# Attention and expert kernel: queries computed transposed for two tiles at a time, rope rows placed by DMA, slots in group order

## The reference

```python
q_c = layernorm(x) @ W_dq                       # 96 values a row
kv_c = ctx @ W_kvc                              # 64 values a key
scores = (q_nope . k_nope + rope(q_rope) . rope(k_rope)) / sqrt(128 + 64)
good = (k <= seg_id) & (k >= seg_id - 8)        # a band of 9 keys
out = softmax(where(good, scores, -1e30)) @ v @ W_o
x = x + out
gate = layernorm(x) @ gate_w + gate_b           # top 2 of 8
x = x + mean of the two relu(layernorm(x) @ expert_w[e] + expert_b[e])
```

## Time and profile before

| | |
|---|---|
| three runs, us | 395.62, 395.87, 397.86; median 395.87 |
| span of the profiled execution, us | 391.2 |
| around it, by the median | 4.7 |
| busy us: PE, PEld, DVE, ACT, POOL | 354.0, 289.2, 288.3, 264.0, 234.1 |
| share of the span | 90%, 74%, 74%, 67%, 60% |

### The profile page before, as it was taken

The page is one execution under the profiler, slowest core; times in us unless marked ns, Lnnn a source line. Parts: engine busy times, 40 slices in busy tenths (PEclk is TensorE's granted clock), DMA queues, the critical chain, the costliest instruction groups (busy, mean ns, idle before and its releaser), DMA issues.

```text
span 391.2 us, 10358 instructions
## 1 busy us (share of the span) xinstructions
PE 354.0 (90%) x2507; PEld 289.2 (74%) x2507; DVE 288.3 (74%) x1395; ACT 264.0 (67%) x907; POOL 234.1 (60%) x326
## 2 busy tenths in 40 slices
PE   1989999998999999999999999999998788999940
PEld 0856877786688878888878888788886577888730
DVE  2367887788888889888788888888889566444455
ACT  1347777788878878778888788788787544445430
POOL 4616555468976777677677676776764355455500
PEclk9999999999999999999999999999999999999985
DMA  8964040000000000000000000000000354543178
GB/s 277 349 215 188 7 105 3 1 3 29 0 30 1 30 20 7 27 0 27 14 14 27 0 27 0 27 27 0 30 2 28 95 161 131 148 132 121 34 239 316
DMA packets 15093, 28.27 MB, mean 72 GB/s; under 512 B 2892, under 2 KB 10719, under 8 KB 14416
## 3 DMA queue, kind: packets, MB, share of 16 engines
q1 hardware_dynamic: 11408, 20.25, 16.1%
q0 software_dynamic: 2960, 6.94, 5.0%
q10 hardware_dynamic: 688, 0.64, 0.6%
HBM read 17.81 MB, written 10.91 MB: 73 GB/s over the span
## 4 chain that ended last, share of the span: by engine, by line
PE 65%; DVE 12%; issue 10%; POOL 7%; DMA 2%; ACT 2%; DVEq 0%; SPq 0%; POOLq 0%; ACTq 0%
PE psum L1133 11%; PE psum L672 8%; PE psum L673 8%; PE psum L674 8%; PE psum L1090 7%; PE psum L1203 6%; PE psum L1117 5%; POOL prob L1361 2%; DVE x_all L1554 2%; POOL q_sb L1347 2%; PE psum L1180 2%; DVE nsc L1622 2%; DMA wcat<-in_w_kvc 2%; PE psum L369 2%; PE psum L1012 1%
## 5 line engine op out<-in xcount | busy, mean ns | idle before, releaser
L1228 ACT ACTIVATE prob<-nsc,nmax 128x128 f32<-128x128 f32 x256 | 100.8, 396 | 36.3 <-DVE nmax L1622 35.5
L1347 POOL TENSOR_TENSOR q_sb<-rope_a,rope_b 128x256 f32<-128x256 f32 x64 | 47.5, 742 | 59.2 <-DVE rope_b L1585 55.1
L1361 POOL TENSOR_TENSOR prob<-prob,prec 128x512 f32<-128x512 f32 x64 | 67.2, 1050 | 7.4 <-DVE prec L1593 7.4
L1133 PE MATMUL psum<-kT_all,qT 128*128 (+1 forms) x512 | 68.6, 277 | 1.1 <-ACT qT L1271 1.1
L1622 DVE CUSTOM_DVE_ANT_0 nsc<-psum,mask 128x128 f32<-128x128 f32 x256 | 58.6, 284 | 13.0 <-PE psum L1133 13.0
L1133 PEld LDWEIGHTS psum<-kT_all,qT 128*128 128x128 f32 x512 | 62.1, 192 | 2.7 <-ACT qT L1271 2.4
L1415 POOL DMA_INDIRECT halves<-jout,jidx x33 | 32.2, 976 | 30.3 <-DVE jidx L1526 13.7
L1228 ACT ACTIVATION_READ_ACCUMULATOR prob<-nsc,nmax 128x1 f32 x256 | 48.4, 189 | 0.0
L1090 PE MATMUL psum<-ident,q_sb 128*128 128x128 f32 x256 | 41.9, 286 | 2.2 <-POOL q_sb L1347 1.8
L1090 PEld LDWEIGHTS psum<-ident,q_sb 128*128 128x128 f32 x256 | 26.8, 140 | 21.7 <-POOL q_sb L1347 13.6
L1203 PE MATMUL psum<-pT,v_cur 128*64 128x256 f32 x256 | 41.8, 405 | 0.0
(11 more groups left out here) (204 smaller groups left out, 878.1 us busy)
## 6 DMA issues: line engine op xcount, KB each, us to landing
wanted<-slots SPq DMA_DIRECT2D x33, 129.0 KB, 2.4
wo_raw<-in_w_o SPq DMA_DIRECT2D x2, 1024.0 KB, 14.9
we_raw<-in_expert_w SPq DMA_DIRECT2D x1, 2048.0 KB, 7.8
half<-halves SPq DMA_DIRECT2D x4, 512.0 KB, 7.1
x_all<-in_x SPq DMA_DIRECT2D x2, 640.0 KB, 17.4
slots<-pad_row SPq DMA_DIRECT2D x8, 129.0 KB, 3.4
we_raw<-in_ctx_near SPq DMA_DIRECT2D x1, 1024.0 KB, 11.2
out<-x_all SPq DMA_DIRECT2D x2, 512.0 KB, 4.6
```

The source lines that it names most:

```text
L1133: mm = pe.matmul(B_S[r][:, h, :], qT[r][:, h, :], batch_keys, start=True, stop=True)
L1228: e = act.activation(prob[r][:, h, :], nsc[r][:, h, :], ACT.Exp, bias=nmax[r][:, h:h + 1], scale=-1.0, accum_out=psum_h[r][:, h:h + 1])
L1347: pool.tensor_tensor(q_sb[1 - r][:, :, KVC:P], rope_a[1 - r][:], rope_b[1 - r][:], ALU.add).then_inc(m["rope_joined"], 1)
L1361: pool.tensor_tensor(p[:], p[:], prec[1 - r][:, :].unsqueeze(2).to_broadcast([P, HG, P]), ALU.mult).then_inc(m["prob_normed"], 1)
```

## The change

The weights of the query product become the stationary operand and the latent rows of both tiles of a batch (256 columns) the moving one, so that queries come out with dims in partitions. QT, its copy and the split copies `qc_hi[j]` go. W_qr's columns are rearranged on the host. A quad is one head group of two tiles: 32 quads, one every two slots. Its rope part is a bank of 2 x 256 columns; DVE multiplies it with a table `ropeT` (384 KB, before `ropeq` 128 KB), POOL adds, and SP, which now walks the slots too, moves the result by eight DMAs of 32 partitions x 256 (32 KB each) into rows 64 to 127 of `qT`. ACT copies the other half with two copies of 64 x 512. Slots go group by group: tiles 2b and 2b+1 alternate; a batch ends with both tiles, and the transposes of their rows start five and nine slots after its last group (before: five after the last group of the tile). PE's order is PT, S, query product, output product, PV. Both tiles' outputs share a bank that one more matmul sets to zero. Walk ends after three further slots; the first four dense pieces stand in slots 65 and 66, all jobs follow, the other eight dense pieces come last.

```diff
@@ PE, queries
+            def q_part(z, g, first):
+                for q in range(2):
+                    cols = q_cols(first + q)
+                    mm = mm3(pe, z[:, L * q:L * q + L], wq_hi[:, g, cols], wq_lo[:, g, cols], qc_hi[:], qc_lo[:])
+                return mm
+            def query(b, k):
...
+                if k % TPB and live(p + 2, QUADS):
...
+                    at_least(pe, "rope_parts", p + 2)
...
+                    q_part(B_R, g, 2).then_inc(m["qr_done"], 1)
+                if k % TPB == 0 and live(p + 1, QUADS):
...
+                    q_part(B_N, g, 0).then_inc(m["qn_done"], 1)
@@ PE, slot
-                if live(i, GROUPS):
-                    at_least(pe, "rope_joined", i + 1)
...
-                    for h in range(HG):
-                        mm = pe.transpose(B_QT[:, P * h:P * h + P], q_sb[r][:, h, :], ident[:])
...
+                if isinstance(i, int) and i == GROUPS + 1:
+                    dense(0)
+                    dense(1)
...
                 if live(i, GROUPS):
-                    at_least(pe, "qT_sb", i + 1)
+                    if t == 0:
+                        at_least(pe, f"qr_put{g % 2}", 128 * (2 * b + g // 2 + 1))
+                        at_least(pe, "nope_copied", 2 * p + 2)
...
+                    if (k - 3) % SLOTS == 0:
+                        pe.matmul(B_Y[:, :], zero16[:], ones16[0:1, :].unsqueeze(1).to_broadcast([1, 4, P]), start=True, stop=False)
...
+                if isinstance(i, int) and i == GROUPS + 2:
+                    dense(2)
+                    dense(3)
+                    first_turns()
@@ DVE, slot
+                if t == 0 and live(p + 1, QUADS):
...
+                    at_least(dve, "qr_done", p + 2)
+                    at_least(dve, f"qr_put{into}", 128 * ((SLOTS // TPB // 2) * b + (k // TPB + 1) // 2))
+                    at_least(dve, "rope_joined", p + 1)
+                    a = B_R.rearrange("p (a n) -> p a n", a=2)
+                    dve.tensor_tensor(rope_c[into][:], a, ropeT[:, 0:1, :].to_broadcast([P, 2, L]), ALU.mult)
+                    dve.tensor_tensor(rope_s[:], a[:, ::-1, :], ropeT[:, 1:3, :], ALU.mult).then_inc(m["rope_parts"], 1)
...
+                if kn == 2 and live(nb - 1, B):
+                    batch_sum(nb - 1)
+                if (kn == 3 or isinstance(i, int) and i == GROUPS + 2) and live(nb - 1, B):
+                    batch_spread(nb - 1)
...
+                if isinstance(i, int) and i == GROUPS:
+                    count_blocks()
+                    experts_of_jobs()
+                if isinstance(i, int) and i == GROUPS + 1:
+                    choose(w)
+                    rows_of_jobs()
+                if isinstance(i, int) and i == GROUPS + 2:
+                    prepare(0)
+                    prepare(1)
...
@@ POOL, slot
+                if k % TPB == 0 and live(pn, QUADS):
+                    into = rope_c[(k // TPB + 1) % 2]
+                    at_least(pool, "rope_parts", pn + 1)
+                    pool.tensor_tensor(into[:], into[:], rope_s[:], ALU.add).then_inc(m["rope_joined"], 1)
                 if live(i - 1, GROUPS):
                     at_least(pool, "recip_done", i)
@@ SP
+            def slot(b, k):
...
+                if k % TPB == 0 and live(pn, QUADS):
+                    at_least(sp, "rope_joined", pn + 1)
+                    at_least(sp, "s_done", 2 * pn - 2)
+                    for h in range(HG):
+                        for a in range(2):
+                            sp.dma_start(qT[into][KVC + QR * a:KVC + QR * a + QR, h, :],
+                                         rope_c[into][QR * h:QR * h + QR, a, :]).then_inc(m[f"qr_put{into}"], 16)
+                if isinstance(i, int) and i == 0:
+                    late_weights(sp, "k_mm")
@@ end
-        JOBS_IN_SLOT = {GROUPS: [0], GROUPS + 1: [2], GROUPS + 2: [4], GROUPS + 3: [5, 6], GROUPS + 4: [7, 8], GROUPS + 5: [9, 10]}
-        DENSE_AFTER_JOB = {8: 0, 11: 1, 14: 2, 17: 3, 20: 4, 23: 5, 26: 6, 29: 7}
+        ROWS_AFTER_JOB = {1: NS + 1, 5: NS + 2}
+        GATE_AFTER_JOB = {3: NS + 1, 7: NS + 2}
+        CHOICE_AFTER_JOB = {4: NS + 1, 8: NS + 2}
...
-                for j in range(JOBS_IN_SLOTS, NJ):
+                for j in range(NJ):
                     job(j)
-                for f in range(2 * GPT, DENSE):
+                for f in range(GPT, DENSE):
                     dense(f)
```

More of the change, by code:

```diff
@@ L48 @@
 SLOTS = TPB * GPT
+QUADS = GROUPS // TPB
+NOPE = HG * KVC
+QR = R // 2
 PAIRS = H // 2
@@ L667, in walk @@
                     slot(b, k)
-            for k in range(SLOTS + 6):
+            for k in range(SLOTS + 3):
                 slot(B - 1, k)
@@ L1070, in late_gate, with row_turn @@
                 mm.then_inc(m["gate_done"], 1)
+            def row_turn(w, j=None):
+                j = w % 2 if j is None else j
+                at_least(pe, "x2n_done", w + 1)
+                at_least(pe, "placed", w if not isinstance(w, int) else min(w, NS))
+                if isinstance(w, int) and w == 0:
+                    pe.wait_ge(m["x_columns"], B - 1)
+                if isinstance(w, int) and w > NS:
+                    pe.wait_ge(m["gate_step"], 6 * (w - 1) + 1)
+                for c in range(DC):
+                    mm = pe.transpose(B_E[:, P * c:P * c + P], row[j][:, P * c:P * c + P], ident[:])
+                mm.then_inc(m["xT_done"], 1)
@@ L1205, in slot @@
                     mm.then_inc(m["pv_done"], 1)
-                if g == 0 and live(t - 2, TILES) and late_turn:
-                    row_turn()
-                for j in jobs_of(i):
-                    job(j)
             pe.wait_ge(S("flag_done"), 1)
@@ L1320, in slot @@
                     wo_high(act, i - 12)
-                if g == 0 and live(t - 2, TILES) and late_turn:
-                    row_high(t, k)
-                for j in jobs_of(i):
-                    job(j)
+                if isinstance(i, int) and i == GROUPS + 2:
+                    for f in range(GPT):
+                        dense(f)
+                    job_high(0)
+                    job_high(1)
             act.wait_ge(S("flag_done"), 1)
@@ L1406, in slot @@
                     pool.wait_ge(S("counted"), 6)
-                if job_between(i) is not None:
-                    job(job_between(i))
-                for j in jobs_of(i):
-                    job(j)
             def job(j):
@@ L1556, in slot, with job @@
+            def job(j):
+                for ahead in next_rows(j):
+                    prepare(ahead)
+                if j in ROWS_AFTER_JOB:
+                    row_low(ROWS_AFTER_JOB[j])
+                if j in CHOICE_AFTER_JOB:
+                    choose(CHOICE_AFTER_JOB[j])
+                if j in (0, 2):
+                    dense(j)
+                    dense(j + 1)
             def slot(b, k):
-                i, g, t = SLOTS * b + k, k % GPT, TPB * b + k // GPT
+                i, t = SLOTS * b + k, k % TPB
+                p = (SLOTS // TPB) * b + k // TPB
+                step, w, j = places(b, k)
@@ L1566, in slot @@
+                if step == 1 and live(w, TILES) and not (isinstance(i, int) and i >= GROUPS):
+                    choose(w, [0, 1])
                 if live(i - 3, GROUPS) and not plain(i - 3):
@@ L1723, in _ @@
             with sp.If(near == 1):
-                late_loads(sp, "k_mm")
-                sp.wait_ge(S("pad_set"), 2)
-                for e in range(NE):
-                    sp.dma_start(slots.ap()[CAP * e:CAP * e + P, :], pad_row[:]).then_inc(S("padded"), 16)
+                walk(sp, slot)
                 sp.wait_ge(S("padded"), 16 * NE)
```

620 lines of the change are left out of this document (305 added, 315 removed).

## The result

The changed kernel takes 414.62 us (median of 4 runs, 412.48 to 417.34), the kernel before 396.81 beside it: ratio 1.047 (95% interval 1.042 to 1.052). It is slower by 4.7%, where 388.0 was forecast. The profiled execution took 416.08 us, its span is 413.9 against 391.2.

A forecast was written before the change was run, and what follows sets the result against it. PE was taken to bound the kernel before, waits for POOL's norm after. -6.1 up to slot 17, +3.6 in five batches, -0.7 and -4.4 at the end make -7.6 on 391.2: 383.6, plus 4.7, said 388; range 370 to 401.

The forecast's parts named there:

- the mechanism: Looped batch: QT's gain is lost to PT waiting for POOL's norm, behind POOL's sum and DVE's rope; +3.6 in all.
- the walk: Looped batch: eight slots followed in order, each engine taking its next operation when free and its input there; 33.9 us a batch.
- rival B: Even slots' S: the rope rows' DMAs are the bound; a batch takes 36, time 401; chance 0.15.
- DVE's small operations on finished rows: Odd slots of a looped batch: they make the next oT_lo up to 0.5 late once or twice.
- The scatters' hold of 3.4 us: Slots 0 and 4 of a batch: the next norm waits 3.4 for POOL, and PT of slots 2 and 6 for it.
- The train: SP's eight DMAs a quad: issues 0.50 apart; up to 0.4 of S's time twice a batch, included as a risk.
- The 2.0 taken for the landing: Rope rows' DMAs: the time a DMA takes to land, taken as 2.0 between 1.8 and 3.4.
- Rival A: Looped batches: PE keeps the pace as DVE and POOL overlap more; batch 30.1 to 32, time 369; chance 0.20.
- Slots 9 to 17: Before the looped batches: POOL's scatters leave as first rows come four slots later; 3.95 a slot, -5.5.
- The opening: Start: S of slot 0 waits for rope rows, to 27.8, +3.8; S of slot 2 at 37.9, +2.3.
- The end: From slot 64: first scatter at 18.8, POOL paces jobs at 1.27, last scatter at 59.8; -4.4 taken.
- The term around the span: Outside the profiled span: 4.7 added to the span of 383.6, giving 388.3.

The follow-up runs named there:

- E9: Changed kernel with rope ahead of choice (slots 1, 5), rank product behind output product, mask ahead of scatters, two DMAs a quad placing other rows than needed: 390.7 us.
- E12: Changed kernel with rope, rank product and mask reordered, ACT issuing four opening DMAs, wcat loaded first, S waiting for rope rows by head pairs: 394.7 us.
- E16: Changed kernel with scatters in two slots, S waiting by head pairs, four opening DMAs issued by ACT, wcat first, constants early: 393.4 us.
- E5: Changed kernel with two DMAs a quad placing other rows than needed, and POOL's mask ahead of the scatters: 400.9 us.
- E15: Changed kernel with one edit, a tile's two scatters issued in two slots instead of one: 405.2 us.
- E1: Changed kernel with two 128 KB DMAs a quad in place of eight of 32 KB, placing other rows than the scores need: 406.5 us.
- E4: Changed kernel with ropeT's load issued behind the contexts, one place later, and POOL's constants ahead of the first sum: 415.8 us.
- E7: Changed kernel with ropeT's load last on ACT's queue, gate_bias in its place on SP, and POOL's constants ahead of the first sum: 414.8 us.
- E10: Changed kernel with rope, rank product and mask reordered, ACT issuing two of eight DMAs in the loop and four in the opening, wcat first: 413.7 us.
- E13: As E12, but S waits once for all eight DMAs instead of by head pairs: 397.8 us.
- E14: E12 with a tile's two scatters issued in two slots instead of one: 394.0 us.

## Why the prediction was wrong

**Half of the mechanism was right.** PE is no longer the bound: busy 86% of a batch (88% forecast). POOL's norm stands behind the sum and some PTs wait for it; the sum takes 1.29 (1.30); in five batches slots 17 to 57 got longer. But the walk had these waits at slots 1, 2, 5, 6 and 7 and of about 4 us a batch in all (33.9, less 30.1 of PE's own work). They are at 3, 6 and 7 and of 2.1 us, the longest at slot 3, which the walk gave to PE. The larger part of PE's idle time, 2.9, is S waiting for DMAs. That is the prediction's own sign of rival B: "S released by DMA in most even slots". With the overlooked waits cured the batch is 33.6 to 34.0 (E9, E12, E16), near the 33.9 of the walk; that is luck as much as proof, since in E16 the waits lie elsewhere.

**The step that failed first: the walk through the eight slots, +14.4 us.** Set beside E5, whose batch of 35.97 has no train and no mask's wait, the walk's PT distances of 4.8, 4.9 and 3.5 for the slots 0 to 1, 1 to 2 and 7 to 0 are right (4.8, 4.9, 3.5); those to slots 3 and 7 are not: 3.5 forecast, 4.6 found, and 3.9, 4.8 found. The other three differ by 0.2 to 0.5 and nearly cancel. Three terms were mis-sized or missing:
- "DVE's small operations on finished rows ... make the next oT_lo up to 0.5 late once or twice." They are 1.3 us ahead of the rope in slots 2 and 6, and one of them is held further. The earlier trace rows were read by durations; what stood in DVE's order in front of the rope was not counted there.
- The scatters' hold of 3.4 us was laid on the norm alone. It also held the mask, through it the maxima, the choice, the rope, the sum and the DMAs. E15 takes most of the hold away for 1.75 us a batch.
- The train: "up to 0.4 of S's time twice a batch". The issues come 0.63 apart, not 0.50, and S can start 6.7 us after the sum at the earliest; it waited 2.9 us a batch. The 2.0 taken for the landing was right (1.9), though the section of the Trainium skill that the prediction cites for it gives its 2.0 for DMAs issued by GpSimd, and these are SP's. The issues were the wrong term. By landing alone B was not to be expected (it "decides from a landing of about 2.5 on"), but by its own sum of cadence and landing, 3.5 + 2.5 = 6.0, it was: 4.4 + 1.9 = 6.3. Still the train was not the only cause: E1 shows that without it the batch stays. Behind the scatters' delay both chains were late by nearly the same, so that taking away the one (E1) let the other through.

Rival B came nearest, with a batch of 36 (36.5 measured) and 401 us; the 14 that it was short are mostly the opening, slots 9 to 17 and the end. No rival had two chains late together. Rival A needed the steps between to overlap more, and they overlapped less.

**Slots 9 to 17, +4.3.** The forecast of 3.95 a slot took only the scatters out. The looped batch's waits are there from slot 12 on: S of 12 waits 0.8 for DMAs, PT of 15 waits 1.7 for POOL.

**The opening, +6.4 up to slot 2.** "DMAs to 22.3 + 3.5 + 2 = 27.8": the sum itself came 2.7 late, as the first product did; from the train's first issue to S it took 7.3 and not 5.5, as the issues are 0.63 apart and one of them took 1.5; and the half clock made S and the keys' product longer (3.11 us for 1.95). That the constants would hold the next sum was seen, but they turned out not to matter (E4).

**The end, +5.4 from slot 57.** From S of slot 57 to slot 64 it took 30.3 us for 28.6, the loop's waits again; the first scatter came 0.9 later than forecast. The jobs ran 1.28 apart, as forecast at 1.27, but only from the twelfth scatter on: the first eleven intervals took 2.9 more. PE had rows and gates of the last tiles between the first jobs (ACT waited for PE, POOL for ACT). No run took these away, so this stands on the trace alone. After the last scatter it took 20.6, for 20 and the 0 to 2 allowed for the eight dense pieces.

**The term around the span**, 4.7: only about 2 of it lie around a span. The rest stands for before's profiled execution, quicker than its median, and after's was not. So the sum misses the span by 30.3 us (413.9 for 383.6) and the time by 26.6.

**Still open** is why the first product starts at 11.5 and not at 8.8. The place of ropeT's load did not do it (E4, E7); no run took its 256 further KB away. With wcat first on ACT's queue it started at 9.1 to 10.5, then waiting for another small load of that queue (E10, E12, E13, E14, E16). That small pieces on one queue are held by large rows on the other would fit, but was not tried by itself.

## What to carry to other kernels

When a full engine is relieved, look for everything that stood in its shadow at once: here a block of POOL work of 2.3 us and seven tiny operations on DVE were harmless at 33.2 us a batch and were not when PE's own work fell to 31.5, and the eight short DMAs that came in place of PE's transposes were late beside them. Follow a hold past the first instruction behind it: on an in-order queue it delays all of them, and the cheap one (a mask of 0.47 us) may be the one that the longest chain needs. When two chains are late by the same amount, an experiment that cures one may show nothing; cure the common cause (split the long block) or both, and only then price each.

## What the hardware showed beyond what was expected

- **DVE held by POOL.** A DVE operation on 8 columns takes 1.0 to 1.8 us for 0.2 where POOL's sum or norm is running, and ends with it:

```profile
247.39 1.00 DVE L1484 TENSOR_SCALAR gt<-logit,top 128x8 f32<-128x8 f32 x1
```

```profile
247.30 1.05 POOL L1405 TENSOR_TENSOR prob<-prob,prec 128x512 f32<-128x512 f32 x1
```

  The same operation takes 0.9 to 1.0 in each of the five looped batches, while row maxima that read PSUM beside POOL's sum keep their 0.29. It is nothing that the change brought; the kernel before has it too, at 0.9 to 1.2 us (DVE, then POOL):

```profile
213.00 1.13 DVE L1452 TENSOR_SCALAR gt<-logit,top 128x8 f32<-128x8 f32 x1
```

```profile
213.05 1.04 POOL L1361 TENSOR_TENSOR prob<-prob,prec 128x512 f32<-128x512 f32 x1
```

  This is coincidence in time, and no run took it away. The Trainium skill (SBUF — State Buffer, SBUF: two separate sides) states a rule for it. By that GpSimd and a DVE operation in a two-port mode, or one with two SBUF inputs where GpSimd reads SBUF too, lock one shared pair of ports for a whole instruction, and the other "fully blocks". The trace agrees in part. TENSOR_SCALAR and TENSOR_TENSOR from SBUF are held beside POOL's sum and norm, and the operations from PSUM are not. But the same kinds of operation keep their 0.17 to 0.3 us beside POOL's TENSOR_SCALAR of the masks, and in E15 and E16 beside a scatter. E1's operation of 1.79 us began beside a scatter too, 0.7 us before the norm with which it ended; why it was held from there on is open.
- **DMAs of 32 KB between SBUF rows** start 0.63 us apart on SP and land 1.9 us after their issue (median; 1.8 to 3.0 over the 128 of 256 for which the trace has a landing). Two of 128 KB in their place land 2.3 after theirs and made the opening's train 4.2 us shorter (E1).
- **An idle PE cost twice**: after 5.1 us without work the granted clock was 0.50, and the next eight matmuls took 2.08 us for 1.16. In E1 S of slot 0 came 4.2 us earlier, and the clock stayed at 1.00.
